# Attention: the scalar engine rounds the output weights in its first slots, the pool keeps their remainders, and the bias is added in pieces of 512 columns

## The chip, the cores and the metric

The kernel runs on one core of one Trainium2 chip. The metric is the device time of one execution in microseconds (us). Five engines work beside one another and meet only at semaphores: PE (matrix multiply), DVE (vector), ACT (scalar), POOL (GpSimd) and SP, which here only issues transfers. Runs of this kernel differ among themselves by about 0.7%.

## The reference, cut to what matters

Two layers, each an attention part and a feed-forward part, on a tensor of 16 batches x 128 rows x 512 columns in float32. The change lies in the attention of layer 1, which comes third of the four parts:

```
q      = rms_norm(x @ q_w + q_b, nq_s)            # 16 heads of 128 columns
k      = rms_norm(ctx @ ki_w + ki_b, nki_s)
v      = ctx @ vi_w + vi_b
attn   = softmax(q k^T / sqrt(128))               # for each batch and head, 128 x 128
x      = x + (attn v) @ o_w + o_b                 # o_w is 2048 x 512
```

The context is shorter than the 257 rows that the reference cuts off as image context, so the text part of it is empty and only the image part is computed.

## The kernel before, in words

Each part of the network is a `Phase`: it allocates its buffers, gives every engine its own program, and ends at a barrier of all engines. The queries, keys and values lie in device memory when the phase `attend` begins (function `attend`, from L2521); the output weights `raw` (16 heads, each 128 x 512) and the bias `obias`, spread over the 128 partitions, are already on the core.

`attend` does 64 steps. Step n = 4*it + j is one head of one group of four batches (`it` runs over 16 quads: four groups g times four quads of heads; j is the head in the quad). What a step does on each engine, and which line it has in the profile:

- DVE `keys` (L2715) scales the keys of a head by a column and by a row, from three buffers on the core; PE `score` (L2793) makes the scores of four batches into a bank; DVE `peak` takes the maximum (L2722) and multiplies it by -rq (L2725, 128 x 4).
- ACT `softmax` (L2675) makes four exponentials of 128 x 128 with their sums; DVE `divide` takes reciprocals (L2732) and scales the probabilities (L2734, 128 x 512).
- PE `turn_prob` (L2801) transposes them, ACT `turned` (L2682) copies them out, PE `mix` (L2812) multiplies with the values.
- The mixed rows are split in a rounded leading part `ol` by ACT `head` (L2688) and the remainder `ot` by DVE `rest` (L2739). PE `output` multiplies them with the output weights in three passes (L100 to L102, twelve matmuls of 512 columns for one batch and one quad), and DVE `add` (L2749) adds the result to `x`.

The stages run displaced, by hand: in the program for step n, PE does transpose(n), mix(n-1), scores(n+2), output(n-5); DVE does add(n-6), keys(n+3), divide(n+1), peak(n+2), rest(n-1); ACT does exponentials(n+1), leading part(n-1), copy(n). Every engine takes its instructions strictly in the order written, and each buffer between two of them is double, so an engine can run at most about two steps ahead. In steps 0 to 4 there is no output to multiply yet.

The weights need the same split, `wol` (rounded, FP32R) and `wot` (the remainder). Before the change POOL does all of it: `cut(i)` is a TENSOR_SCALAR times 1.0 (L2642), then a TENSOR_TENSOR subtraction (L2644), for 16 heads. After four cuts POOL adds the bias to the four batches of group 0 in one instruction of 2048 columns (L2650), then come twelve cuts, then the bias of the three other groups. PE waits for `wo_ready` (four cuts each) ahead of the first output of a quad, and DVE waits for `bias_done` ahead of the first add of a group. The first output is in step 5, the first add that needs the bias of group 1 in step 22.

Of the kernel before, what the change touches and what calls it, by code (L numbers as in the profile page):

```python
# [20 lines left out]
ALU = mybir.AluOpType  # L21
ACT = mybir.ActivationFunctionType
AX = mybir.AxisListType.X

P = 128
B, S, D = 16, 128, 512
T = B * S
C = D // P
GB = 4
# [32 lines left out]
class Phase:  # L62
# [15 lines left out]
    def sb(self, name, shape, dt=F32):  # L78
        return self.stack.enter_context(self.nc.sbuf_tensor(f"{self.name}_{name}", shape, dt))

    def sem(self, name):
        self.sems.append(self.nc.alloc_semaphore(name=f"{self.name}_{name}"))
        return self.sems[-1]
# [2437 lines left out]
def attend(nc, K, A, q_dram, k_dram, v_dram, rq, rk_dram):  # L2521
# [7 lines left out]
    with Phase(nc, "attend") as ph:  # L2529
        sb, sem = ph.sb, ph.sem  # L2530
        raw = A.raw
        wol = sb("wol", [P, H1, D], F32R)
# [4 lines left out]
        kcol, qcol, vbias, obias = A.kcol, A.qcol, A.vbias, A.obias  # L2537
# [8 lines left out]
        wol_done, wo_ready, rkb_loaded = sem("wol_done"), sem("wo_ready"), sem("rkb_loaded")  # L2546
        bias_done, col_done = sem("bias_done"), sem("col_done")
# [6 lines left out]
        def group(it):  # L2554
            return it >> 2 if isinstance(it, int) else within(nc, it >> 2, G - 1)

        def quad_of(it):
            return it & 3 if isinstance(it, int) else within(nc, it & 3, QUADS - 1)
# [4 lines left out]
        def blocks(eng, body):  # L2563

            body(0, 0)
            body(1, 1)
            with eng.Fori(1, IT // 2 - 1) as i:
                body(i * 2, 0)
                body(i * 2 + 1, 1)
            body(IT - 2, 0)  # L2570
            body(IT - 1, 1)

        def ahead(it, par, j, d, step):

            q, k = divmod(j + d, 4)
            if not isinstance(it, int) or 0 <= it + q < IT:
                step(it + q, (par + q) % 2, k)
# [61 lines left out]
        @block.gpsimd  # L2639
        def _(pool):  # L2640
            def cut(i):
                nc.gpsimd.tensor_scalar(wol[:, i], raw[:, i], 1.0, None, ALU.mult).then_inc(wol_done, 1)  # L2642
                pool.wait_ge(wol_done, i + 1)
                ins = nc.gpsimd.tensor_tensor(wot[:, i], raw[:, i], wol[:, i].bitcast(F32), ALU.subtract)  # L2644
                if i % 4 == 3:
                    ins.then_inc(wo_ready, 1)

            def bias(g):
                xg = K.x[:, g * GB:(g + 1) * GB, :]
                nc.gpsimd.tensor_tensor(xg, xg, obias[:].unsqueeze(1).broadcast_to([P, GB, D]), ALU.add  # L2650
                                        ).then_inc(bias_done, 1)

            for i in range(4):
                cut(i)
            bias(0)
            for i in range(4, H1):
                cut(i)
            pool.wait_ge(wo_ready, QUADS)
            pool.sem_inc(wo_ready, IT - QUADS)
            for g in range(1, G):  # L2660
                bias(g)

        @block.scalar
        def _(act):
            for first in (exp_done, probT_done,):
                act.sem_inc(first, FIRST)
            nc.scalar.activation(K.scrap[:], K.ones[:, 0:1], ACT.Exp)

            def softmax(it, j):
                n, g = it * 4 + j, group(it)  # L2670
                act.wait_ge(max_done, n + 1)
                ph.hold(act, held_act)

                for b in range(GB):
                    ins = nc.scalar.activation(prob[:, j % 2, b, :], ps[:, j % 2, b * S:(b + 1) * S], ACT.Exp,  # L2675
                                               bias=row[:, j % 2, 1, b:b + 1], scale=rq[:, bass.ds(g * GB + b, 1)],
                                               accum_out=row[:, j % 2, 2, b:b + 1])
                ins.then_inc(exp_done, 1)

            def turned(it, j):  # L2680
                act.wait_ge(prob_T, it * 4 + j + 1)
                nc.scalar.activation(probT[:, j % 2, :], ps[:, 2 + j % 2, :], ACT.Copy).then_inc(probT_done, 1)  # L2682

            def head(it, par, j):
                act.wait_ge(mixed, it * 4 + j + 1)
                ph.hold(act, held_act)

                nc.scalar.activation(ol[:, par, j, :], ps[:, 4 + j % 2, :], ACT.Identity,  # L2688
                                     bias=vbias[:, bass.ds(quad_of(it) * 4 + j, 1)]).then_inc(ol_done, 1)

            def body(it, par):
                for j in range(4):
                    ahead(it, par, j, 1, lambda i, p, k: softmax(i, k))
                    ahead(it, par, j, -1, head)
                    turned(it, j)

            softmax(0, 0)
            blocks(act, body)
            head(IT - 1, 1, 3)
            row_stats.root(act)  # L2700
# [292 lines left out]
```

## Time and profile before

| | us |
|---|---|
| median of three runs | 1539.83 |
| lowest and highest of them | 1533.41, 1544.79 |
| the profiled execution: time | 1534.74 |
| the profiled execution: span | 1532.3 |
| phase `attend` in it, first instruction to last matmul | about 1120 to 1471 |
| POOL at work in that phase | 1120.2 to 1190.9 |

The profile gives, for one execution, every instruction with start and length; a line in brackets behind an instruction is the idle time of the engine before it and who ended it. PE is busy for 90% of the span, DVE for 55%, ACT for 49%, POOL for 28%. Since the phases stand one after the other, what matters in one phase is how long that phase lasts. The start of `turn_prob` (L2801) in each step is a good clock of the phase: below, T(n) is the start of the first transpose of step n.

### The profile page before, as it was taken

How to read it: one execution, taken by the hardware profiler on the slowest of the kernel's cores; microseconds unless marked ns; L12 is line 12 of the kernel's file. 1: busy time of each engine (PE TensorE's matmuls, PEld its weight loads, DVE VectorE, ACT ScalarE, POOL GpSimd, SP SyncE). 2: the span in 40 equal slices, each digit the busy share in tenths (PEclk: the TensorE clock that was granted, in tenths of full speed). 3: DMA queues.
4: the chain of work that ended last, by engine and by line, in shares of the span. 5: the costliest groups of instructions: out<-in, count | busy, mean ns of one | idle time of the engine just before them, and what ended most of it. 6: DMA issues, size and time to landing. Idle time of an engine off the chain costs nothing. (4 is left out here: it accounts for less than half of the span.)

```text
span 1532.3 us, 26058 instructions
## 1 busy us (share of the span) xinstructions
PE 1377.8 (90%) x7406; PEld 1141.4 (74%) x7407; DVE 836.0 (55%) x1544; ACT 754.1 (49%) x1845; POOL 424.1 (28%) x367
## 2 busy tenths in 40 slices
PE   6899998999898969979999939999958899999968
PEld 5786676888787758857886627878857788888856
DVE  2432322367667875444444247723259777777673
ACT  4222223588678745125555534545435565666520
POOL 0110102236364800539922043020079000000004
PEclk9999998799999977989999969999979999999988
DMA  6998245887787610356645775463445455555202
GB/s 233 356 352 316 108 138 180 290 274 253 234 265 264 220 56 28 137 173 202 195 140 162 246 235 159 144 234 131 160 131 156 144 156 164 159 165 156 70 35 110
DMA packets 171764, 280.91 MB, mean 183 GB/s; under 512 B 29664, under 2 KB 64224, under 8 KB 171424
## 3 DMA queue, kind: packets, MB, share of 16 engines
q1 hardware_dynamic: 146832, 227.58, 46.4%
q0 software_dynamic: 7712, 26.22, 5.1%
q10 hardware_dynamic: 17136, 26.09, 4.6%
q8 instruction: 40, 0.66, 0.2%
q14 instruction: 44, 0.36, 0.1%
HBM read 173.14 MB, written 106.70 MB: 183 GB/s over the span
## 5 line engine op out<-in xcount | busy, mean ns | idle before, releaser
L2675 ACT ACTIVATE attend_prob<-banks,attend_row,rq 128x128 f32<-128x128 f32 x256 | 113.7, 454 | 68.9 <-DVE attend_row L2725 68.9
L100 PE MATMUL banks<-of_shared_split,heads_wl 128*128 (+1 forms) x256 | 108.5, 424 | 17.4 <-ACT heads_ksq L944 12.2
L100 PE MATMUL banks<-of_shared_split,of_ctx_lead 128*128 128x512 f32 x256 | 106.2, 415 | 9.3 <-DVE of_ctx_trail L419 5.5
L100 PE MATMUL banks<-attend_wol,attend_ol 128*128 (+1 forms) x256 | 105.6, 413 | 0.0
L100 PE MATMUL banks<-of_x_lead,queries_wl 128*128 128x512 f32 x256 | 101.9, 398 | 3.8 <-ACT queries_sq L2342 2.3
L102 PE MATMUL banks<-of_shared_split,heads_wt 128*128 (+1 forms) x256 | 103.2, 403 | 0.0
L102 PE MATMUL banks<-of_shared_split,of_ctx_trail 128*128 128x512 f32 x256 | 103.2, 403 | 0.0
L101 PE MATMUL banks<-of_shared_split,of_ctx_lead 128*128 128x512 f32 x256 | 102.9, 402 | 0.0
L2884 POOL TENSOR_TENSOR x_kept<-x_kept,ternary_bias 128x2048 f32 x4 | 18.2, 4594 | 305.6 <-DVE ternary_trail L1298 305.6
L101 PE MATMUL banks<-of_shared_split,heads_wl 128*128 (+1 forms) x256 | 102.6, 401 | 0.0
L101 PE MATMUL banks<-of_x_trail,queries_wl 128*128 128x512 f32 x256 | 101.1, 395 | 0.0
L102 PE MATMUL banks<-of_x_lead,queries_wt 128*128 128x512 f32 x256 | 101.0, 395 | 0.0
L102 PE MATMUL banks<-attend_wol,attend_ot 128*128 (+1 forms) x256 | 100.5, 393 | 0.0
L101 PE MATMUL banks<-attend_wot,attend_ol 128*128 (+1 forms) x256 | 100.1, 391 | 0.0
L2414 DVE TENSOR_TENSOR queries_total<-queries_total,queries_sq 128x512 f32<-128x512 f32 x60 | 41.7, 696 | 91.4 <-ACT queries_sq L2342 91.3
L2338 ACT ACTIVATE queries_head<-banks,queries_bias 128x512 f32<-128x512 f32 x64 | 44.0, 688 | 96.1 <-PE banks L102 84.1
L1053 DVE TENSOR_TENSOR heads_total<-heads_total,heads_ksq 128x512 f32 (+1 forms) x64 | 60.7, 948 | 54.0 <-ACT heads_ksq L944 53.7
L892 ACT ACTIVATE heads_dec<-mlstm_gmax,mlstm_nat 128x128 f32<-128x128 f32 x264 | 83.3, 389 | 5.8 <-POOL mlstm_gmax L794 5.8
L2749 DVE TENSOR_TENSOR x_kept<-x_kept,banks 128x512 f32 (+1 forms) x64 | 43.9, 686 | 67.7 <-PE banks L102 65.0
L2688 ACT ACTIVATE attend_ol<-banks,of_attend_vbias 128x512 fp32r<-128x512 f32 x64 | 44.0, 688 | 73.7 <-PE banks L2812 73.5
L1160 PEld LDWEIGHTS banks<-heads_ctx,heads_cmat 128*128 128x128 f32 x512 | 72.0, 210 | 8.6 <-POOL heads_ctx L803 3.1
L2793 PE MATMUL banks<-attend_kn,attend_q 128*128 128x128 f32 x512 | 70.9, 284 | 5.4 <-DMA attend_q<-q_heads 5.4
(329 smaller groups left out, 3635.8 us busy)
## 6 DMA issues: line engine op xcount, KB each, us to landing
mlstm_gmax<-running_max SPq DMA_DIRECT2D x36, 512.0 KB, 5.8
heads_raw<-in_L_xattn_ki_w SPq DMA_DIRECT2D x32, 512.0 KB, 6.0
k_heads<-heads_key ACTq DMA_DIRECT2D x64, 256.0 KB, 4.2
q_heads<-queries_head SPq DMA_DIRECT2D x64, 256.0 KB
attend_q<-q_heads SPq DMA_DIRECT2D x64, 256.0 KB
of_attend_k<-k_heads SPq DMA_DIRECT2D x60, 256.0 KB, 4.1
of_attend_v<-v_heads SPq DMA_DIRECT2D x60, 256.0 KB, 3.2
sorted_rows<-values_zeros SPq DMA_DIRECT2D x2, 5120.0 KB, 18.2
```

What stands on the lines that cost most here:

```text
L100: nc.tensor.matmul(out, lead_l, lead_r, start=first, stop=False)
L101: nc.tensor.matmul(out, lead_l, trail_r, start=False, stop=False)
L102: return nc.tensor.matmul(out, trail_l, lead_r, start=False, stop=last)
L892: ins = nc.scalar.activation(dec[:, n % 2, b], gmax[:, h // 2 % 4, h % 2 * N + b * S:h % 2 * N + (b + 1) * S], ACT.Exp, scale=-1.0, bias=M ...
L1053: nc.vector.tensor_tensor(t, t, ksq[:, m % 2, :], ALU.add).then_inc(total_done, 1)
L1160: ins = nc.tensor.matmul(ps[:, n // 2 % 2, at:at + DH0 + 1], cmat[:, n % RING, b, :], ctx1[:, bass.ds(half(g), 1), b, n, :].rearrange("p a ...
L2338: nc.scalar.activation(head[:, u % HEADS_RING, :], ps[:, u % 4, :], ACT.Identity, bias=bias[:, h:h + 1]).then_inc(head_done, 1)
L2414: nc.vector.tensor_tensor(t, t, sq[:, u % 2, :], ALU.add).then_inc(total_done, 1)
L2675: ins = nc.scalar.activation(prob[:, j % 2, b, :], ps[:, j % 2, b * S:(b + 1) * S], ACT.Exp, bias=row[:, j % 2, 1, b:b + 1], scale=rq[:, b ...
L2688: nc.scalar.activation(ol[:, par, j, :], ps[:, 4 + j % 2, :], ACT.Identity, bias=vbias[:, bass.ds(quad_of(it) * 4 + j, 1)]).then_inc(ol_do ...
L2749: nc.vector.tensor_tensor(xb, xb, ps[:, 6 + b % 2, :], ALU.add).then_inc(acc_done, 1)
L2793: ins = nc.tensor.matmul(ps[:, j % 2, s], q[:, j, s], kn[:, j % 2, s], start=True, stop=True)
```

## The change

ACT makes the rounded weights: four of them behind the load of its function table, ahead of its first exponentials; two at the end of each of steps 0 to 3; one at the end of each of steps 4 to 7. POOL waits for each and makes only the remainders. The bias is added in 16 instructions of 512 columns each instead of four of 2048; its semaphore is still raised once for each group.

```diff
         @block.gpsimd
         def _(pool):
             def cut(i):
-                nc.gpsimd.tensor_scalar(wol[:, i], raw[:, i], 1.0, None, ALU.mult).then_inc(wol_done, 1)
                 pool.wait_ge(wol_done, i + 1)
                 ins = nc.gpsimd.tensor_tensor(wot[:, i], raw[:, i], wol[:, i].bitcast(F32), ALU.subtract)
                 if i % 4 == 3:
                     ins.then_inc(wo_ready, 1)
 
             def bias(g):
-                xg = K.x[:, g * GB:(g + 1) * GB, :]
-                nc.gpsimd.tensor_tensor(xg, xg, obias[:].unsqueeze(1).broadcast_to([P, GB, D]), ALU.add
-                                        ).then_inc(bias_done, 1)
+                for b in range(g * GB, (g + 1) * GB):
+                    ins = nc.gpsimd.tensor_tensor(K.x[:, b, :], K.x[:, b, :], obias[:], ALU.add)
+                ins.then_inc(bias_done, 1)
...
+            def weight_lead(i):
+                nc.scalar.activation(wol[:, i], raw[:, i], ACT.Copy).then_inc(wol_done, 1)
+
             def body(it, par):
                 for j in range(4):
                     ahead(it, par, j, 1, lambda i, p, k: softmax(i, k))
                     ahead(it, par, j, -1, head)
                     turned(it, j)
-
+                    if isinstance(it, int) and it < 2:
+                        for i in ((4 + 2 * j, 5 + 2 * j), (12 + j,))[it]:
+                            weight_lead(i)
+
+            for i in range(4):
+                weight_lead(i)
             softmax(0, 0)
             blocks(act, body)
```

ACT at the start of `attend`, before the change (the exponentials are the row `attend_prob`, eight of them for steps 0 and 1):

```order
L2667 ACT_TABLE_LOAD
L2667 ACTIVATE scrap<-ones 128x1
L2675 ACTIVATE attend_prob,attend_row<-banks,attend_row,rq 128x128 x8
L2682 ACTIVATE attend_probT<-banks 128x512
L2675 ACTIVATE attend_prob,attend_row<-banks,attend_row,rq 128x128 x4
L2688 ACTIVATE attend_ol<-banks,of_attend_vbias 128x512
L2682 ACTIVATE attend_probT<-banks 128x512
L2675 ACTIVATE attend_prob,attend_row<-banks,attend_row,rq 128x128 x4
```

The same place now (lines below the edit have moved by up to seven):

```order
L2666 ACT_TABLE_LOAD
L2666 ACTIVATE scrap<-ones 128x1
L2691 ACTIVATE attend_wol<-of_attend_raw 128x512 x4
L2674 ACTIVATE attend_prob,attend_row<-banks,attend_row,rq 128x128 x8
L2681 ACTIVATE attend_probT<-banks 128x512
L2691 ACTIVATE attend_wol<-of_attend_raw 128x512 x2
L2674 ACTIVATE attend_prob,attend_row<-banks,attend_row,rq 128x128 x4
L2687 ACTIVATE attend_ol<-banks,of_attend_vbias 128x512
L2681 ACTIVATE attend_probT<-banks 128x512
L2691 ACTIVATE attend_wol<-of_attend_raw 128x512 x2
```

Four rounded weights now stand ahead of the first exponentials, and two behind each copy `attend_probT` of the first four steps.

POOL's whole program of the phase before began with these rows (alternating in this way for all 16 heads):

```order
L2642 TENSOR_SCALAR attend_wol<-of_attend_raw 128x512
L2644 TENSOR_TENSOR attend_wot<-of_attend_raw,attend_wol 128x512
L2642 TENSOR_SCALAR attend_wol<-of_attend_raw 128x512
L2644 TENSOR_TENSOR attend_wot<-of_attend_raw,attend_wol 128x512
L2642 TENSOR_SCALAR attend_wol<-of_attend_raw 128x512
L2644 TENSOR_TENSOR attend_wot<-of_attend_raw,attend_wol 128x512
L2642 TENSOR_SCALAR attend_wol<-of_attend_raw 128x512
L2644 TENSOR_TENSOR attend_wot<-of_attend_raw,attend_wol 128x512
L2650 TENSOR_TENSOR x_kept<-x_kept,of_attend_obias 128x2048
L2642 TENSOR_SCALAR attend_wol<-of_attend_raw 128x512
L2644 TENSOR_TENSOR attend_wot<-of_attend_raw,attend_wol 128x512
```

and is now, in full:

```order
L2643 TENSOR_TENSOR attend_wot<-of_attend_raw,attend_wol 128x512 x4
L2649 TENSOR_TENSOR x_kept<-x_kept,of_attend_obias 128x512 x4
L2643 TENSOR_TENSOR attend_wot<-of_attend_raw,attend_wol 128x512 x12
L2649 TENSOR_TENSOR x_kept<-x_kept,of_attend_obias 128x512 x12
```

The 16 instructions L2642 are gone from POOL; all that is left there are instructions with two input tensors, and none is longer than 512 columns.

## Rows read from the trace of the kernel before

**Rows 1.** The page: busy time, share and count of each engine.
```profile
PE 1377.8 (90%) x7406; PEld 1141.4 (74%) x7407; DVE 836.0 (55%) x1544; ACT 754.1 (49%) x1845; POOL 424.1 (28%) x367
```

**Rows 2.** Waits, 1120 to 1475: waiter, releaser, total us, times, longest.
```profile
PE banks L2801 <- DVE attend_prob L2734: 19.6, 8, 5.1
```

**Rows 3.** Windows: stretch, length, busy PE, PEld, DVE, ACT, POOL; PE clock; DMA.
```profile
1180.00:1190.00 10.00, 5.20 (x32) 4.35 (x32) 9.96 (x6) 2.93 (x10) 10.00 (x3) 1.00 0.18 57
1300.00:1400.00 100.00, 100.00 (x645) 88.84 (x644) 72.94 (x142) 60.83 (x200) 0.00 (x0) 1.00 0.58 160
```

**Rows 4.** Timeline of PE, transposes of steps 0,1,2,5,6,9 to 12: start, us, idle before.
```profile
1130.22 1.09 PE L2801 MATMUL banks<-ident,attend_prob 128*128 128x128 f32 x4 [2.95 <-DVE attend_prob L2734]
...
1137.95 1.11 PE L2801 MATMUL banks<-ident,attend_prob 128*128 128x128 f32 x4 [4.93 <-DVE attend_prob L2734]
...
1143.02 1.08 PE L2801 MATMUL banks<-ident,attend_prob 128*128 128x128 f32 x4 [0.54 <-DVE attend_prob L2734]
...
1154.42 0.66 PE L2801 MATMUL banks<-ident,attend_prob 128*128 128x128 f32 x4 [1.35 <-DVE attend_prob L2734]
...
1159.47 0.60 PE L2801 MATMUL banks<-ident,attend_prob 128*128 128x128 f32 x4
...
1174.46 0.60 PE L2801 MATMUL banks<-ident,attend_prob 128*128 128x128 f32 x4
...
1182.09 0.66 PE L2801 MATMUL banks<-ident,attend_prob 128*128 128x128 f32 x4 [2.50 <-DVE attend_prob L2734]
...
1192.35 1.12 PE L2801 MATMUL banks<-ident,attend_prob 128*128 128x128 f32 x4 [5.06 <-DVE attend_prob L2734]
...
1198.70 0.60 PE L2801 MATMUL banks<-ident,attend_prob 128*128 128x128 f32 x4
```

**Rows 5.** Timeline of DVE: instructions that lie beside POOL's.
```profile
1126.59 0.23 DVE L2725 SCALAR_TENSOR_TENSOR attend_row<-attend_row,rq 128x4 f32<-128x4 f32 x1
1126.74 0.74 DVE L2715 SCALAR_TENSOR_TENSOR attend_kn<-of_attend_k,of_attend_kcol,of_attend_rkb 128x512 f32<-128x512 f32 x1
...
1130.80 1.09 DVE L2725 SCALAR_TENSOR_TENSOR attend_row<-attend_row,rq 128x4 f32<-128x4 f32 x1
1131.81 5.07 DVE L2715 SCALAR_TENSOR_TENSOR attend_kn<-of_attend_k,of_attend_kcol,of_attend_rkb 128x512 f32<-128x512 f32 x1
...
1177.18 4.85 DVE L2734 TENSOR_TENSOR attend_prob<-attend_prob,attend_row 128x512 f32<-128x512 f32 x1
...
1182.67 3.81 DVE L2725 SCALAR_TENSOR_TENSOR attend_row<-attend_row,rq 128x4 f32<-128x4 f32 x1
```

**Rows 6.** Timeline of POOL, same stretches.
```profile
1126.19 1.49 POOL L2642 TENSOR_SCALAR attend_wol<-of_attend_raw 128x512 fp32r<-128x512 f32 x1
...
1130.58 1.29 POOL L2644 TENSOR_TENSOR attend_wot<-of_attend_raw,attend_wol 128x512 fp32r<-128x512 f32 x1
1131.83 4.50 POOL L2650 TENSOR_TENSOR x_kept<-x_kept,of_attend_obias 128x2048 f32<-128x2048 f32 x1
...
1181.45 9.49 POOL L2650 TENSOR_TENSOR x_kept<-x_kept,of_attend_obias 128x2048 f32<-128x2048 f32 x2
```

**Rows 7.** Groups, 1200 to 1475, POOL idle: count, busy us, mean ns, idle before.
```profile
L2734 DVE TENSOR_TENSOR attend_prob<-attend_prob,attend_row 128x512 f32<-128x512 f32 x51 | 35.3, 691 | 1.7
L2725 DVE SCALAR_TENSOR_TENSOR attend_row<-attend_row,rq 128x4 f32<-128x4 f32 x50 | 8.1, 162 | 3.6 <-DVE attend_row L2722 1.1
```

**Rows 8.** Timeline of ACT: phase start; a later step's exponentials; rounding in another phase.
```profile
1120.29 1.28 ACT L2667 ACT_TABLE_LOAD   x1 [1.59 <-PEq L76]
...
1126.94 0.46 ACT L2675 ACTIVATE attend_prob<-banks,attend_row,rq 128x128 f32<-128x128 f32 x1 [5.15 <-DVE attend_row L2725]
...
1155.29 0.46 ACT L2675 ACTIVATE attend_prob<-banks,attend_row,rq 128x128 f32<-128x128 f32 x1 [0.87 <-DVE attend_row L2725]
...
319.99 0.63 ACT L928 ACTIVATE heads_wl<-heads_raw 128x512 fp32r<-128x512 f32 x1 [0.22 <-issue]
```

**Rows 9.** Groups, 364 to 510: another addition of 512 columns on POOL.
```profile
L839 POOL TENSOR_TENSOR x_kept<-x_kept,heads_sq 128x512 f32 x10 | 14.9, 1506 | 0.0
```

## The prediction, made before the changed kernel ran

> **What bounds the kernel now.** I read the page first: PE is busy for 90% of the span [rows 1], so only time in which PE stands still can be won. The change touches one phase, so the next view is the table of windows over that phase. From 1200 on PE is full (100.00 of 100.00 us) at the full granted clock, which is 2.4 GHz, while DVE has 27 us in 100 to spare and POOL does nothing [rows 3]; nothing can be won there. In 1180 to 1190 it is the other way round: PE 5.20, DVE 9.96, POOL 10.00 of 10 us [rows 3]. The list of waits names one wait of PE that matters: for the scaled probabilities of DVE, eight times, 19.6 us in all, the longest 5.1 [rows 2].
>
> The timeline of PE shows where. With T(n) the start of the transposes of step n [rows 4]: T(0) 1130.22, T(1) 1137.95, T(2) 1143.02, T(5) 1154.42, T(6) 1159.47, T(9) 1174.46, T(10) 1182.09, T(11) 1192.35, T(12) 1198.70. So a step takes (1154.42 - 1143.02)/3 = 3.80 us where no output is multiplied yet. That is the loop peak, exponentials, divide, next peak, over DVE and ACT; PE waits in it. It takes (1174.46 - 1159.47)/3 = 5.00 us where PE multiplies the output too and is itself the bound. Two stretches stand out: T(0) to T(2) and T(9) to T(12).
>
> The timelines of DVE and POOL, laid side by side, say why. An instruction of DVE with two inputs on the core stands still while POOL runs one with two inputs. The keys L2715 take 0.74 alone, but 5.07 from 1131.81, beside a bias of 4.50 from 1131.83: 4.33 of blocking, nearly its whole length. L2734 takes 0.69 alone [rows 7] and 4.85 from 1177.18; L2725 takes 0.16 alone [rows 7] and 3.81 from 1182.67 [rows 5, 6]. Beside the subtraction of 1.29 from 1130.58, L2725 takes 1.09 from 1130.80: it ends when that does, so a subtraction blocks for about 1.15. Beside the TENSOR_SCALAR from 1126.19, the keys from 1126.74 take their plain 0.74, and L2725 from 1126.59 takes 0.23, 0.07 more than alone [rows 5, 6]: an instruction of DVE that starts 0.4 to 0.6 us into the one-input instruction is hardly held up by it. So what hurts most is the bias, and what the change takes off POOL is the milder half of a cut.
>
> **The change, part by part.**
>
> *The late biases, T(9) to T(12).* Before: 1198.70 - 1174.46 = 24.24 us against three steps at 5.00, so 9.24 lost. The last part of it is PE's clock: after PE stood idle 5.06 us the four transposes of step 11 took 1.12 against 0.60 or 0.66, the lower level of 1.2 GHz. After: twelve pieces. The nearest row for a piece is the POOL addition of 512 columns of another phase, 1.51 us in the mean [rows 9]; a quarter of the bias of 4.50 would be 1.13 [rows 6]. I take 1.26, near the subtraction's 1.29 of the same size in the same phase. Does DVE get in between two pieces? Two biases ran back to back from 1181.45, and the L2734 that had waited since 1177.18 ended at 1182.03, 0.58 into the first of them [rows 5, 6]; so the one that waits is served at the border, and POOL starts again behind it. In each step DVE has three instructions with two such inputs (L2715, L2734, L2725; 0.74 + 0.69 + 0.16 = 1.59 together), and it is busy for 72.94% of 5.00 = 3.65 us [rows 3]. So 2.06 us of other work, which is not blocked, lies beside the three pieces that start behind them: 3 x 1.26 - 2.06 = 1.7 of waiting a step. With it DVE takes 5.35, 0.35 over PE's 5.00, for the 3.6 steps that twelve pieces last (12 x 1.26 = 15.1, and 0.6 to 0.8 a step while POOL itself waits): 1.3 us. Ahead of it stands slack: at T(10) a block of 4.16 cost PE only 7.63 - 5.00 = 2.63, so 1.5 us were absorbed, which covers that. I take a loss of 0.5; the ends are 0, and three full waits of 1.26 in 3.6 steps, 3.6 x (3.65 + 3.78 - 5.00) - 1.5 = 7.2. **Term: -8.7** (-9.2 to -2.0).
>
> *Up to T(0).* ACT is idle for 5.15 us ahead of its first exponential [rows 8], and four roundings of 0.63, as the copy of that kind and size in another phase takes [rows 8], are 2.5: nothing. POOL's first subtraction waits for the table load, which ends at 1121.57 [rows 8], the scrap of 0.2 and one rounding: it starts at about 1122.4, some 2 us behind POOL's start before. From there one subtraction follows the other to 1127.6, then four pieces to about 1132.7. The L2725 of step 0, from 1126.59, fell beside a TENSOR_SCALAR and will fall beside a subtraction (+0.9 of its 1.15), and the first L2734 meets a piece (+0.2 over what it met before). **Term: +1.1** (0 to two full blocks, +2.3).
>
> *T(0) to T(1).* Before 7.73, since the keys stood 4.33 us behind the bias [rows 4, 5]. The keys now find a piece of 1.26, most of it beside the exponentials, and L2725 waits 0.5. I take 4.4: **-3.3**. The ends: the free step of 3.80 (-3.9), and three full waits, 3.80 + 3.8 = 7.6 (-0.1).
>
> *T(1) to T(5).* Before 1154.42 - 1137.95 = 16.47, of it 5.07 for the first step (tail of the same jam) and three times 3.80. Two things come here. ACT has 0.87 us idle ahead of the exponentials of a 3.80 step [rows 8] and gets two roundings, 1.26: up to +0.4 in each of four steps, unless the step is longer anyway. POOL gets both subtractions of a step at once, when ACT has done its roundings, about when DVE does L2725. The first then meets the keys, which lie beside the exponentials and have time; the second follows the keys and meets L2734, which is in the loop: 0 to 1.15, I take 0.5. PE is partly at its lower clock here (the transposes of steps 0 to 2 take 1.08 to 1.11 [rows 4]), which lengthens the scores that the loop may wait for; I don't add it, since it lies beside the others. A step is then 3.80 + 0.2 + 0.5 = 4.5. 4 x 4.5 = 18.0: **+1.5**. The ends: four free steps, 15.2 (-1.3); two full subtractions in each, 4 x (3.80 + 2.58) = 25.5 (+9.0).
>
> *Steps 5 to 8.* One rounding and one subtraction a step. The loop needs 3.80 and the PE 5.00, so 1.15 of blocking fits. Nothing. The waits for the weights are covered: the first output is in step 5, its four cuts are done by 1127.5; quad 3 is first used in step 17, its cuts are done in step 8. The same for the bias of group 1 (first needed in step 22, done by about step 12). SP's queue is not touched.
>
> Sum: -8.7 + 1.1 - 3.3 + 1.5 = **-9.4 us**, with ends of -14.4 and +9.2. The profiled execution took 1534.74 and would take 1525.3. It stands 5.1 below the median of 1539.83; from the median it is 1530.4. I give 1530.
>
> **A rule weighed against the rows.** The row of the keys beside the TENSOR_SCALAR showed 0.74, no blocking. The Trainium skill ("SBUF — State Buffer", section "SBUF: two separate sides") says that DVE and GpSimd share one pair of ports under an exclusive lock, and that a GpSimd instruction that reads SBUF keeps it for the whole instruction against a DVE instruction with two SBUF inputs. With the bias and the subtraction the trace agrees (4.33 of 4.50, about 1.15 of 1.29); with the TENSOR_SCALAR it does not. By the page every cut would have held DVE for 1.49 + 1.29 = 2.78 us before and 1.29 after, so the third and fifth terms could only fall; by the rows two subtractions in a step block more than the mixed pair did. I go by the rows; the other reading is rival A.
>
> **The rivals.**
>
> *A, the start gets shorter too.* If POOL's pair of subtractions slips beside the exponentials as the mixed pair did, steps 1 to 4 keep 3.80: sum -9.2 + 0.5 - 3.9 - 1.3, about -14, or -12 with half of it. Time 1526 to 1528. For it: the cuts before cost next to nothing at 3.80. Against it: they held DVE only about half as long. The page above speaks for it. 13%.
>
> *B, the late pieces still jam DVE.* With pieces of 1.51, as the nearest addition took [rows 9], and 3.0 of waiting a step, DVE takes 6.65, which is 1.65 x 3.6 = 5.9 over PE's pace, less 1.5 of slack: 4.4 lost. That makes -9.2 + 4.4 - 0.7 = -5.5, and -4.1 if PE's clock falls again (step 11 and 12 lost 1.4 by it: 6.35 against 5.00 [rows 4]): 1534 to 1536. Against it: the other work of DVE covers part of each wait. 22%.
>
> *C, slower.* The two subtractions of a step enter the loop in full, because POOL now starts in a burst right behind ACT rather than in its own rhythm: +9.0 in T(1) to T(5) with +2.3 ahead, -0.1, and half of the late gain kept (-4.6). That is +6.6, 1546. It decides from where a step of that stretch takes over 6.0. Against it: the first of the pair meets the keys, which have time. 9%.
>
> *D, nothing to be seen*, -2 to +2, from a start that costs 7: inside B's and C's ranges, counted there.
>
> That leaves 56% for the forecast, -6 to -12.
>
> **How the numbers follow.** The three runs of before lie 11 us apart, so about 1% (15 us) is what a measurement of this kernel can tell from no change. The largest gain that the rows allow, 14.4, is under it, so faster by over 1% needs rival A and luck in the runs: 0.11. Slower by over 1% needs rival C at its end and beyond: 0.04. Within 1%: 0.85. Range: from rival A counted from the profiled execution, 1534.74 - 14.4 = 1520, to rival B counted from the median with the spread of a few us on top, 1541; it leaves out C and the tails.
>
> **What would show each step.** The list of waits: L2801 for L2734 from 19.6 us to about 9. The longest L2715, L2734 and L2725 under 2.5 us each, where they were 5.07, 4.85 and 3.81. T(9) to T(12) near 15.5. T(0) about 1 us later, T(1) near 1135.7, T(5) near 1154, T(12) near 1189. POOL's work over by about 1186, with busy time of 40 instead of 70. A L2734 over 1.3 us in each of steps 1 to 4 would confirm the second subtraction; T(1) to T(5) under 16 is rival A, over 21 rival C; windows of PE under 9 in 10 after T(8) are rival B. Wrong altogether: if the keys, L2734 and L2725 stay over 3 us, the border between two pieces does not let DVE in.

## The result, and the profile after

Over 20 runs of each kernel the change takes 1534.26 us (1525.84 to 1544.45) against 1539.24 (1533.41 to 1547.26): a ratio of 0.9962, 95% interval 0.9945 to 0.9979, or 5.9 us less (3.2 to 8.5); the two medians alone lie 5.0 apart. A second series, of twelve runs, gave 0.9933 (0.9905 to 0.9961). The kernel is faster, by less than 1%. The forecast was 1530, between 1520 and 1541.

The execution of the change that was profiled took 1544.45 us, more than the median of before. Its phase `attend` began at 1135.80 (table load of ACT), where it had begun at 1120.29: 15.5 us were lost ahead of the first changed instruction, by the differences between runs. So the two spans can't be compared, but the phases can. All times of phases below are counted from P, the start of that table load: T(63)-P, the start of the last transposes, was 332.0 before and is 326.6 after, 5.4 less. In these two executions that is what the change does; what a phase gains differs from trace to trace, as the table below shows.

The page after, the same waits as in [rows 2], and the windows from P to T(63) of both kernels, before first (columns as in [rows 3]):

```profile
PE 1387.7 (90%) x7406; PEld 1149.7 (75%) x7407; DVE 833.6 (54%) x1544; ACT 762.8 (49%) x1861; POOL 396.5 (26%) x363
```

```profile
PE banks L2808 <- DVE attend_prob L2741: 15.7, 8, 7.6
```

```profile
1120.29:1452.30 332.01, 308.92 (x1957) 274.64 (x1958) 248.98 (x440) 193.53 (x639) 69.13 (x36) 0.97 0.53 149
```

```profile
1135.80:1462.40 326.60, 307.29 (x1957) 272.79 (x1958) 243.91 (x440) 201.67 (x655) 43.70 (x32) 0.97 0.54 151
```

POOL's busy time falls from 69.1 to 43.7 us, ACT's grows by 8.1 (16 roundings), and DVE's falls by 5.1 though it does the same: DVE's "busy" holds time in which it stands blocked. PE's longest wait for the scaled probabilities has grown, from 5.1 to 7.6.

PE's transposes after, which answer to [rows 4] (steps 0, 1, 2, 5, 6, 9, 10, 11, 12):

```profile
1150.78 1.11 PE L2808 MATMUL banks<-ident,attend_prob 128*128 128x128 f32 x4 [7.61 <-DVE attend_prob L2741]
1154.51 0.66 PE L2808 MATMUL banks<-ident,attend_prob 128*128 128x128 f32 x4 [0.91 <-DVE attend_prob L2741]
1158.89 0.66 PE L2808 MATMUL banks<-ident,attend_prob 128*128 128x128 f32 x4 [1.93 <-DVE attend_prob L2741]
...
1171.98 0.66 PE L2808 MATMUL banks<-ident,attend_prob 128*128 128x128 f32 x4 [0.20 <-DVE attend_prob L2741]
1177.34 0.60 PE L2808 MATMUL banks<-ident,attend_prob 128*128 128x128 f32 x4
...
1192.31 0.60 PE L2808 MATMUL banks<-ident,attend_prob 128*128 128x128 f32 x4
1197.87 0.66 PE L2808 MATMUL banks<-ident,attend_prob 128*128 128x128 f32 x4 [0.43 <-DVE attend_prob L2741]
1203.72 0.66 PE L2808 MATMUL banks<-ident,attend_prob 128*128 128x128 f32 x4 [0.65 <-DVE attend_prob L2741]
1208.75 0.60 PE L2808 MATMUL banks<-ident,attend_prob 128*128 128x128 f32 x4
```

T(9) to T(12) went from 24.24 to 16.44. T(0)-P went the other way, from 9.93 to 14.98. DVE's rows say why (they answer to [rows 5]; the first is step 0, the others lie beside the late pieces):

```profile
1142.23 5.57 DVE L2732 SCALAR_TENSOR_TENSOR attend_row<-attend_row,rq 128x4 f32<-128x4 f32 x1
...
1188.40 1.84 DVE L2722 SCALAR_TENSOR_TENSOR attend_kn<-of_attend_k,of_attend_kcol,of_attend_rkb 128x512 f32<-128x512 f32 x1
...
1190.36 1.58 DVE L2741 TENSOR_TENSOR attend_prob<-attend_prob,attend_row 128x512 f32<-128x512 f32 x1
...
1192.70 0.40 DVE L2732 SCALAR_TENSOR_TENSOR attend_row<-attend_row,rq 128x4 f32<-128x4 f32 x1 [0.16 <-DVE attend_row L2729]
```

and POOL's beside them, which answer to [rows 6]:

```profile
1137.89 5.01 POOL L2643 TENSOR_TENSOR attend_wot<-of_attend_raw,attend_wol 128x512 fp32r<-128x512 f32 x4 [82.19 <-ACT attend_wol L2691]
1142.85 4.93 POOL L2649 TENSOR_TENSOR x_kept<-x_kept,of_attend_obias 128x512 f32<-128x512 f32 x4
...
1187.19 17.60 POOL L2649 TENSOR_TENSOR x_kept<-x_kept,of_attend_obias 128x512 f32<-128x512 f32 x12 [0.18 <-POOLq L2658]
```

The small L2732 of step 0 was asked for at 1142.23, in the last remainder, and ended at 1147.80, with the last of the four pieces (1142.85 + 4.93 = 1147.78). It was let in at none of the four borders between; this is the lock-out of what follows. Beside the late pieces, each of the three instructions waits for one border only: 1.1, 0.9 and 0.2 us.

### The profile page after: what moved, and what is told of

It reads as the page before. It is cut to its first block and busy times, and to the rows that moved or that the text cites. A ratio compares the mean times of both kernels' runs of the same rounds, so it can differ in the third digit from the quotient of the medians.

```text
span 1542.4 us, 26070 instructions
## 1 busy us (share of the span) xinstructions
PE 1387.7 (90%) x7406; PEld 1149.7 (75%) x7407; DVE 833.6 (54%) x1544; ACT 762.8 (49%) x1861; POOL 396.5 (26%) x363
## 5 line engine op out<-in xcount | busy, mean ns | idle before, releaser
L100 PE MATMUL banks<-of_shared_split,heads_wl 128*128 (+1 forms) x256 | 110.2, 430 | 20.3 <-ACT heads_ksq L944 15.4
L101 PE MATMUL banks<-of_shared_split,heads_wl 128*128 (+1 forms) x256 | 104.0, 406 | 0.0
L1043 DVE TENSOR_TENSOR heads_wt<-heads_raw,heads_wl 128x512 fp32r<-128x512 f32 x64 | 60.1, 939 | 31.4 <-ACT heads_wl L928 31.0
```

The lines of the kernel that those rows point to most:

```text
L100: nc.tensor.matmul(out, lead_l, lead_r, start=first, stop=False)
L101: nc.tensor.matmul(out, lead_l, trail_r, start=False, stop=False)
L1043: nc.vector.tensor_tensor(wt[:, m % 2], raw[:, m // 2 % 2, :, (m % 2) * P:(m % 2 + 1) * P], wl[:, m % 2].bitcast(F32), ALU.subtract).then_ ...
```

## The experiments

The theory from these rows: the pieces win T(9) to T(12); the start loses 5 us because DVE can be shut out over a whole series of POOL instructions that follow each other without a gap; the roundings on ACT bring nothing. Twelve more traces, one table. T(0)-P is the time up to the first transposes, T(63)-P the whole phase, all in us. T(16) to T(63) is the same in all but e6 and e8 and shows how well traces compare:

| kernel | T(0)-P | T(0) to T(5) | T(5) to T(9) | T(9) to T(16) | T(16) to T(63) | T(63)-P |
|---|---|---|---|---|---|---|
| before | 9.93 | 24.20 | 20.04 | 44.21 | 233.62 | 332.0 |
| e12 before again | 9.93 | 24.22 | 20.02 | 45.35 | 233.62 | 333.1 |
| the change | 14.98 | 21.20 | 20.33 | 36.40 | 233.65 | 326.6 |
| e1 change again | 10.60 | 22.21 | 21.64 | 36.41 | 233.65 | 324.5 |
| e10 change again, timed | 10.58 | 21.51 | 20.16 | 36.41 | 233.65 | 322.3 |
| e4 waits between pieces | 14.97 | 21.87 | 21.67 | 36.44 | 233.64 | 328.6 |
| e2 whole bias | 14.57 | 21.20 | 25.11 | 39.66 | 233.65 | 334.2 |
| e11 bias first | 10.45 | 21.53 | 20.15 | 36.45 | 233.65 | 322.2 |
| e7 POOL held at start | 10.16 | 22.87 | 21.72 | 36.42 | 233.65 | 324.8 |
| e3 pieces only | 9.91 | 22.23 | 20.22 | 36.82 | 233.65 | 322.8 |
| e9 pieces only, timed | 9.93 | 21.71 | 20.04 | 35.87 | 233.62 | 321.2 |
| e6 gated, POOL rounds | 10.69 | 21.17 | 20.00 | 36.38 | 234.66 | 322.9 |
| e8 gated at the wrong place | 10.45 | 23.42 | 21.09 | 40.14 | 234.71 | 329.8 |
| e5 gated | 9.26 | 19.61 | 20.03 | 34.92 | 233.65 | 317.5 |

**e1, the change once more.** No edit.

> The changed kernel once more, for the start of the phase attend. With P the start of the table load of ACT in the phase and T(n) the start of the transposes of step n, the first trace had T(0)-P 14.98 us, because the first L2732 of DVE, asked for at 1142.23, ran only when all four pieces of the first bias were through (5.57 us). Theory A (POOL keeps the ports over back-to-back instructions at this place, every time): L2732 again over 5 us, T(0)-P about 15. Rival B (chance of arrival: as in all other places DVE is let in at the first border): L2732 under 1.3 us and T(0)-P about 11. T(12)-P: 73 by A, 69 by B.

B, at this place: L2732 took 0.94, T(0)-P 10.60. But e2 and e4, run beside it, which begin on POOL with the same four remainders, had it shut out again. So the start of the change has two outcomes. e4 and e1 asked for L2732 at the same 6.18 us after P and had the fourth remainder from 5.83 and 5.82 on. In e1 it went in at the border:

```profile
1135.47 0.94 DVE L2732 SCALAR_TENSOR_TENSOR attend_row<-attend_row,rq 128x4 f32<-128x4 f32 x1
1136.34 1.83 DVE L2722 SCALAR_TENSOR_TENSOR attend_kn<-of_attend_k,of_attend_kcol,of_attend_rkb 128x512 f32<-128x512 f32 x1
```

and in e4 (L2733 there) at none:

```profile
1130.79 5.81 DVE L2733 SCALAR_TENSOR_TENSOR attend_row<-attend_row,rq 128x4 f32<-128x4 f32 x1
1136.53 0.74 DVE L2723 SCALAR_TENSOR_TENSOR attend_kn<-of_attend_k,of_attend_kcol,of_attend_rkb 128x512 f32<-128x512 f32 x1
```

T(12)-P was 70.9, between the 73 and 69 of the two: there is a second toss, PE's clock. The windows of step 5, e1 first (6.66 us) and then e10 (5.18), show PE's granted clock at 0.74 and 1.00 (last but two columns):

```profile
1162.10:1168.76 6.66, 6.66 (x32) 6.12 (x33) 5.58 (x9) 4.87 (x17) 2.59 (x2) 0.74 0.63 161
```

```profile
1157.46:1162.64 5.18, 5.18 (x33) 4.56 (x33) 4.37 (x8) 3.67 (x12) 1.29 (x1) 1.00 0.71 190
```

PE stands idle for 1.8 to 2.2 us ahead of each of steps 2 to 4 in the trace of the change, and in every trace but that of e10 it is at the lower level (1.2 GHz) for a stretch somewhere in steps 1 to 5; what that costs depends on where. In the trace of the change the stretch lies in step 4, where the granted clock was 0.60 and PE had time to spare:

```profile
1167.72 1.11 PE L2808 MATMUL banks<-ident,attend_prob 128*128 128x128 f32 x4 [2.15 <-DVE attend_prob L2741]
```

That step took no longer (4.26). In e1, e4 and e7 it lies in step 5, the first in which PE is itself the bound, and cost 1.5 to 1.6 us against e10. In e1 and e4 PE was at the lower level in step 1 as well (granted clock 0.50 in e1, 1.00 in e10), and step 2 took 4.96 in place of 4.24, 0.7 us that came with it. So the phase is 322.3 with neither toss against it (e10), 324.5 with the clock alone (e1), 326.6 with the lock-out alone (the change), 328.6 with both (e4).

**e2, the bias whole again.** In `bias(g)`:

```diff
-                for b in range(g * GB, (g + 1) * GB):
-                    ins = nc.gpsimd.tensor_tensor(K.x[:, b, :], K.x[:, b, :], obias[:], ALU.add)
-                ins.then_inc(bias_done, 1)
+                xg = K.x[:, g * GB:(g + 1) * GB, :]
+                nc.gpsimd.tensor_tensor(xg, xg, obias[:].unsqueeze(1).broadcast_to([P, GB, D]), ALU.add
+                                        ).then_inc(bias_done, 1)
```

> The changed kernel with the bias of a group in one instruction of 2048 columns again; the roundings stay on ACT. By my theory the pieces are what wins T(9) to T(12), so that stretch goes back to 22 to 25 us from 16.4. The start: if POOL keeps the ports until its queue of instructions is empty (A), T(0)-P stays about 15; if DVE is let in ahead of the bias (B), T(0)-P is 11 and T(0) to T(1) is 7 to 8. Total against the changed kernel: +6 to +8 us. A rival says that taking the roundings off POOL is what wins; then the total stays within 2 us of the changed kernel.

334.2, 7.6 over the change with the same lock-out at the start: the forecast size. So the roundings alone, with the bias whole, are 1 to 2 us slower than the kernel before, the lock-out included, by one trace of it and two of before. The jam came back, one step earlier than before because POOL is done with its cuts sooner; so T(9) to T(12) (19.7) misses what I said, and T(8) to T(12) shows it, 29.7 against 21.4. PE in step 9 (idle 4.81) and DVE beside the biases:

```profile
1191.46 1.12 PE L2808 MATMUL banks<-ident,attend_prob 128*128 128x128 f32 x4 [4.81 <-DVE attend_prob L2741]
```

```profile
1186.63 4.78 DVE L2741 TENSOR_TENSOR attend_prob<-attend_prob,attend_row 128x512 f32<-128x512 f32 x1
...
1192.16 3.65 DVE L2732 SCALAR_TENSOR_TENSOR attend_row<-attend_row,rq 128x4 f32<-128x4 f32 x1 [0.16 <-DVE attend_row L2729]
```

**e3 and e9, pieces only.** In the kernel before; e9 is the same kernel, timed beside e10, the change.

```diff
-                xg = K.x[:, g * GB:(g + 1) * GB, :]
-                nc.gpsimd.tensor_tensor(xg, xg, obias[:].unsqueeze(1).broadcast_to([P, GB, D]), ALU.add
-                                        ).then_inc(bias_done, 1)
+                for b in range(g * GB, (g + 1) * GB):
+                    ins = nc.gpsimd.tensor_tensor(K.x[:, b, :], K.x[:, b, :], obias[:], ALU.add)
+                ins.then_inc(bias_done, 1)
```

> The kernel before with only the bias cut in pieces; POOL still makes roundings and remainders in turn. Theory: T(0)-P as before (9.9, since DVE gets in beside the roundings), T(0) to T(1) about 4.5 instead of 7.7, T(1) to T(5) about 15.5, T(9) to T(12) about 16.5 instead of 24.2: T(12)-P about 67, against 78.4 before and 72.9 with the change, so better than the whole change by some 5 us. Rival: the roundings on POOL prolong its work so that the pieces meet DVE as badly; T(12)-P over 72.

> The kernel before with only the bias in pieces, the kernel of e3 once more, timed. In the traces its phase attend (T(63)-P) took 322.8 us against 332.0 before and 324.5 to 328.6 with the whole change. Theory: the pieces are all of the gain and the roundings on ACT cost 2 to 4 us: ratio to before 0.994 (-9 us), at or under that of the change. Rival (the roundings on ACT contribute): ratio over that of the change by 0.002 or more.

322.8 and 321.2 us of phase, against 322.3 to 328.6 with the whole change; measured ratios to before 0.9901 (0.9864 to 0.9937) for the pieces alone and 0.9933 (0.9905 to 0.9961) for the change beside it. Both ratios rest on the same runs of before, so their overlap does not settle which kernel is better. Run against run, the pieces alone were the shorter in 62 of 72 pairs (medians 1524.62 and 1529.54), which chance alone gives in 1 to 2 of 100 cases: the roundings on ACT cost time here. By the traces they cost it mainly where DVE is shut out; without that the phases are alike (322.3 in e10 against 322.8 and 321.2). T(12)-P in e3 was 68.3 where I had said 67, since steps 0 to 5 still took 22.2. T(9) to T(12) says little here: POOL's late pieces come later, and what they cost falls on steps 11 and 12 (5.88 and 5.86 in e3), of which step 12 lies outside that stretch.

**e4, waits between the pieces.** In the loop of `bias(g)`:

```diff
+                    pool.wait_ge(wol_done, 4)
                     ins = nc.gpsimd.tensor_tensor(K.x[:, b, :], K.x[:, b, :], obias[:], ALU.add)
```

> The changed kernel with a wait of POOL on a semaphore that is long there ahead of each piece of the bias. If DVE was shut out in the first bias because the pieces follow each other without a gap (A), the first L2732 falls from 5.57 to under 1.5 us and T(0)-P to about 11. If the gap does not matter (rival), it stays over 5. T(9) to T(12) within 0.5 us of 16.4 in both cases.

The rival came: 5.81. A wait that is already met makes no gap; the pieces start 1.22 us apart with it as without it.

**e10, the change timed.** No edit.

> The changed kernel beside e9 on the same chip. Theory: ratio 0.996; in its trace DVE's first L2732 is either shut out over the whole series of eight back-to-back POOL instructions (over 5 us, T(0)-P about 15) or let in at the first border (under 1 us, T(0)-P 10.6), nothing in between.

Let in (0.83), ratio 0.9933 where I had 0.996. In five traces that begin with four remainders and the bias (the change, e1, e2, e4, e10) L2732 took 5.1 to 5.8 us three times and 0.8 to 0.9 twice, and nothing lay between. The blocking also goes the other way: where DVE is let in, POOL's next piece takes 1.71 in place of 1.26, 0.45 longer (here the second piece of e10).

```profile
1133.63 1.71 POOL L2649 TENSOR_TENSOR x_kept<-x_kept,of_attend_obias 128x512 f32<-128x512 f32 x1
```

**e11, bias first.**

```diff
+            bias(0)
             for i in range(4):
                 cut(i)
-            bias(0)
```

> The changed kernel with the four pieces of the first bias ahead of the first four remainders. The pieces need no rounding, so POOL starts at once, beside the first two keys. If DVE can be shut out over any back-to-back series (theory), the keys or the first L2732 may wait up to 5 us, T(0)-P between 10 and 16, and the long wait ends within 0.1 us of the last POOL instruction of the series. If only the change of kind from remainder to piece does it (rival), no wait over 1.3 us and T(0)-P 10 to 12.

The rival's numbers came: the two first keys took 3.38 in place of 1.42, about 1.0 of waiting each, L2732 took 0.72, and T(0)-P was 10.45. But DVE is let in by chance too, in two of five of the traces above, so one run does not show that the order of the kinds decides. What makes POOL keep the ports stays open.

**e7, POOL held at the start.** Ahead of POOL's first cut:

```diff
+            pool.wait_ge(max_done, 1)
             for i in range(4):
                 cut(i)
```

> The changed kernel with one wait ahead of POOL's first instruction, until DVE's first L2732 is done. The first trace of the change and two of three experiments had DVE shut out over all back-to-back instructions there (5.1 to 5.8 us). Theory: with POOL idle at that moment the first L2732 takes 0.2 and is never shut out; the first four remainders and pieces move some 4.5 us later, onto steps 0 to 2. T(0)-P 10 to 11 instead of 15. T(63)-P about 323 to 325. Rival (DVE gets shut out by the next back-to-back series in the same way): one of keys, scaling or L2732 over 4 us in steps 0 to 2.

The theory held: no wait over 1.1 us anywhere, T(0)-P 10.16, T(63)-P 324.8, which includes the dip of the clock in step 5 (6.76). The gain at the start is given back in part in steps 0 to 4 (22.9), where now every scaling waits about 0.5.

**e5, gated.** POOL's program becomes a list: four cuts, four pieces, twelve cuts, twelve pieces, each behind DVE's L2732 of one step; ACT's roundings 4 to 15 spread over steps 0 to 7.

```diff
-            for i in range(4):
-                cut(i)
-            bias(0)
...
+            for m, step, i in plan:
+                pool.wait_ge(max_done, m + 1)
+                step(i)
...
-                        for i in ((4 + 2 * j, 5 + 2 * j), (12 + j,))[it]:
+                        for i in ((4 + j,), (8 + 2 * j, 9 + 2 * j))[it]:
```

> The changed kernel, with each POOL instruction of the phase held back until DVE has just finished the L2732 (here by its line of this kernel) of a certain step: one a step, from step 0 to 30 (two in step 9); ACT makes its roundings 4 to 15 one, then two a step. Theory (an instruction of POOL costs only if it meets L2732 or the scaling of the probabilities; behind L2732 it meets only the keys, which have time): T(0)-P 9.4, steps 0 to 4 about 3.85, T(9) to T(12) 15.0, T(63)-P about 318 against 332.0 before, 326.6 in the first trace of the change and 324.5 in the second: about -14 us against before. Rival (each POOL instruction costs the same wherever it starts, or POOL's late work costs outputs): T(63)-P not under 323.

317.5, forecast 318. It has the shortest phase of all and the lowest ratio, 1519.24 us against 1538.93, 0.9885 (0.9841 to 0.9929, from four runs; the interval overlaps that of the pieces alone). DVE in it, one step of 3.73 us, with POOL's piece behind it:

```profile
1148.84 0.69 DVE L2742 TENSOR_TENSOR attend_prob<-attend_prob,attend_row 128x512 f32<-128x512 f32 x1
1149.45 0.68 DVE L2730 TENSOR_REDUCE attend_row<-banks 128x4 f32<-128x512 f32 x1
1150.17 0.16 DVE L2733 SCALAR_TENSOR_TENSOR attend_row<-attend_row,rq 128x4 f32<-128x4 f32 x1
1150.25 0.74 DVE L2747 SCALAR_TENSOR_TENSOR attend_ot<-banks,of_attend_vbias,attend_ol 128x512 fp32r<-128x512 f32 x1
1150.91 1.32 DVE L2723 SCALAR_TENSOR_TENSOR attend_kn<-of_attend_k,of_attend_kcol,of_attend_rkb 128x512 f32<-128x512 f32 x1
```

```profile
1150.41 1.28 POOL L2648 TENSOR_TENSOR x_kept<-x_kept,of_attend_obias 128x512 f32<-128x512 f32 x1 [2.45 <-DVE attend_row L2733]
```

The piece takes DVE 0.6 us, on the keys (1.32 for 0.74), beside ACT's exponentials, where it costs nothing.

**e8, gated at the wrong place.** Against e5:

```diff
-                pool.wait_ge(max_done, m + 1)
+                pool.wait_ge(exp_done, FIRST + m + 1)
```

> As the gated kernel, but each POOL instruction is released by the end of ACT's exponentials instead of DVE's L2732, so that it starts just ahead of the scaling of the probabilities. Theory: the scaling waits about 1.0 in every step and it lies in the loop, so steps 0 to 4 take 4.7 to 4.9 instead of 3.85; from step 5 on PE is the bound and the wait is absorbed; T(63)-P 4 to 5 us over the gated kernel. Rival: placement is indifferent, within 1 us of the gated kernel.

POOL now starts 0.17 us ahead of the scaling, which takes 1.65 for 0.69:

```profile
1156.51 1.65 DVE L2742 TENSOR_TENSOR attend_prob<-attend_prob,attend_row 128x512 f32<-128x512 f32 x1
```

```profile
1156.34 1.26 POOL L2648 TENSOR_TENSOR x_kept<-x_kept,of_attend_obias 128x512 f32<-128x512 f32 x1 [3.42 <-ACT attend_prob L2675]
```

Steps 0 to 4 took 4.69 each against 3.92 in the mean in e5. The same instructions cost 3.8 us more there, and 1.2 more up to T(0), by where they start: together 5.0, where 4 to 5 was forecast. The total is 12.3 over e5, because my list held POOL's work so late that others waited for it. In step 6 DVE's first add waited 2.73 us for the first bias (1.0 us lost), and in steps 9, 13 and 17 PE waited for weights (4.1, 1.2 and 1.1 us lost). Step 9 took 9.05 us, with 2.21 idle ahead of its output and a granted clock of 0.81:

```profile
1188.57 0.50 PE L100 MATMUL banks<-attend_wol,attend_ol 128*128 x1 [2.21 <-issue]
```

The first part is the test; the second is a flaw of the list.

**e6, gated, with POOL rounding.** The kernel before with the list of e5. Against e5:

```diff
             def cut(i):
+                nc.gpsimd.tensor_scalar(wol[:, i], raw[:, i], 1.0, None, ALU.mult).then_inc(wol_done, 1)
                 pool.wait_ge(wol_done, i + 1)
...
-                        for i in ((4 + j,), (8 + 2 * j, 9 + 2 * j))[it]:
-                            weight_lead(i)
...
-            for i in range(4):
-                weight_lead(i)
```

> The same holding back, but in the kernel before, with POOL making both rounding and remainder of each weight and the bias in pieces; ACT has nothing added. Theory: the remainder now starts 1.6 us behind L2725 and can meet the scaling of the probabilities, +0 to +0.5 in four steps: T(63)-P 318 to 320. If moving the roundings to ACT was worth anything, this kernel is over 2 us slower than the gated one with ACT; if not, within 2.

322.9, 5.4 over e5 where 318 to 320 was forecast; ratio 0.9915 (0.9883 to 0.9948), which overlaps that of e5. Of the 5.4, 3.0 lie up to T(5) and belong to the test. The remainder of a weight now starts 2.0 us later than POOL's release (1.6 in step 3), into the scaling (POOL, then DVE):

```profile
1142.29 1.92 POOL L2642 TENSOR_SCALAR attend_wol<-of_attend_raw 128x512 fp32r<-128x512 f32 x1 [1.43 <-DVE attend_row L2726]
1144.30 1.28 POOL L2644 TENSOR_TENSOR attend_wot<-of_attend_raw,attend_wol 128x512 fp32r<-128x512 f32 x1
```

```profile
1144.44 1.70 DVE L2735 TENSOR_TENSOR attend_prob<-attend_prob,attend_row 128x512 f32<-128x512 f32 x1
```

The other 2.4 are the flaw of e8 again: PE waited for weights in steps 9 and 17 (1.18 and 0.78 idle ahead of the output).

```profile
1186.20 0.49 PE L100 MATMUL banks<-attend_wol,attend_ol 128*128 x1 [1.18 <-issue]
```

So with this list the rounding on ACT is worth about 3 us at the start. A list that gates POOL's rounding and its remainder apart, so that each remainder starts right behind L2732, was not tried and could make up for it.

**e12, before again.**

> The kernel before once more, since all gains are counted from one trace of it. Theory (its phase is set by the order of the instructions, not by chance): T(63)-P within 1.5 us of 332.0, with the jams again at T(0) to T(1) (7.7) and T(9) to T(12) (24.2). Rival: its first trace was a bad one like the first of the change, and T(63)-P is 327 or less; then the gain of every kernel here is smaller by as much.

333.1, with both jams (7.73 and 25.4; step 11 took 7.49 instead of 6.35, with PE's granted clock at 0.66 instead of 0.78). The base of the comparison holds.

## Why the prediction was right or wrong

*What bounds the phase, and the late biases: right.* Forecast for T(9) to T(12) -8.7, measured -7.8: 1.44 us were lost where I took 0.5, since steps 9 and 10 took 0.56 and 0.85 over their 5.00. Both parts of that term were a little off. DVE waited 2.0, 2.2 and 2.3 us in steps 8 to 10 where I had 1.7 a step, which with its 3.65 of work is 2.4 us over PE's pace and not 1.3. About 1.0 of that was absorbed, not 1.5: I had read the slack from the one block of 4.16, but DVE waited 5.05 in all in that step of the kernel before. e2 confirms the cause: with the bias whole the jam is back, 7.6 us.

*T(0) to T(1): right where DVE was let in*, 4.06 and 4.07 in e10 and e1, where I had 4.4 and the keys did meet a piece (1.82 and 1.83). The 3.73 of the change's own trace is luck: the pieces were over by then, and the keys ran at 0.74. *T(1) to T(5): near*, 17.47 in the trace of the change and 17.45 in e10 where I had 18.0; 18.1 in e1 and e4, at PE's lower clock. The mechanism (two remainders at once, the second onto the scaling) is in the rows, but at +0.4 in every second step and with L2732 as often its victim. The sign that I had set for it, a scaling of over 1.3 us in each of steps 1 to 4, did not come: in the change's trace the longest took 1.09.

*Up to T(0): wrong in the first trace.* I gave +1.1 with an upper end of +2.3 and measured +5.05. The step that failed is "the one that waits is served at the border". I took it from one border, between two biases, and it holds for every wait of the late pieces (none over 1.1 us); but at the start of the phase it failed in three of five traces. The Trainium skill ("SBUF — State Buffer", section "SBUF: two separate sides") has the lock held for one whole instruction; by that the small L2732 would have waited for the rest of one remainder, 0.7 us. The 0.8 and 0.7 of e1 and e10 agree; the 5.4 of the change does not. Where DVE was let in, the term was +0.65 and the phase 9.7 us shorter (e10, 322.3 against 332.0: -7.8, +0.65, -3.7, +1.0 and +0.1 for the stretches), against -9.4 forecast. The other sign that failed with this step is the list of waits: 15.7 us in place of 19.6, where I had about 9, since 7.6 of it is the wait ahead of T(0). The measured 5.9 lies between that and the 5.4 to 3.4 of the traces with the lock-out (the change, e4). How often each occurs among the untraced runs is not known. That 1534.26 lies within the range is in part luck: the upper end of 1541 was set for late pieces that jam (rival B), and not for a lock-out ahead of T(0).

*Steps 5 to 8: I gave nothing.* 0.1 to 0.3 us in the change and e10, but 1.6 in e1 and e4, nearly all of it in step 5 at PE's lower clock. I had named the clock only for the late jam.

*ACT's idle time:* the roundings start 0.52 us apart (1.17 for two) and fill the pause; behind those of steps 1 and 3 the exponentials follow without one. Where that happens they start 0.24 behind L2732 in place of 0.12, so the cost was under 0.2 a step.

*The rivals.* A (the start gets shorter too) did not come about by itself; e5 shows that it was there to be had, at 14.5 us. The total landed at B's figure (-5.5), but not by B's way: it asked for late waits of 3.0 a step and 4.4 us lost there; they were 2.2 a step, and 1.4 lost. C did not come about, though e8 makes a mild form of it on purpose (4.69 a step, not over 6.0). The roundings, which the change moves to ACT, are not what wins: the pieces win. Moving the roundings was worth something in one comparison alone, 3.0 us where POOL's starts are placed (e6 against e5).

## What to carry to other kernels

Where two engines block each other, count where each instruction of the one starts against the loop of the other, not how long it is in all: the same instructions on POOL cost next to nothing (e5) or 0.8 us more a step (e8). Hold a helper engine back with a semaphore of the engine that it blocks, so that it starts just behind the loop's last critical instruction, and don't let it run a series without gaps ahead of a first critical instruction (holding it back gave T(0)-P 10.16 in e7, against 14.6 to 15.0 in the traces with the lock-out). Such a list must still meet every later deadline: in e6 and e8 it did not, and that cost 2.4 and 7.3 us. When the effect is smaller than the spread of runs, compare a stretch inside the traces from a common point, and take the trace more than once.

## What the hardware showed that I had not expected

DVE's small L2732 (0.16 us) stood 5.1 to 5.8 us behind a series of back-to-back POOL instructions in three traces of five, to the end of the series, from start positions that let it in after 0.7 to 0.8 in the two others. Why is open. A wait on a semaphore that is already met leaves no gap for it (e4, pieces 1.22 us apart with and without). A TENSOR_SCALAR of POOL (1.49 us) holds up two-input instructions of DVE at its start alone: the scaling that began 0.06 us into it took 0.43 longer, the first small instruction of the phase (L2707), at 0.2 us, took 0.27 longer, L2725 at 0.39 us 0.07 longer, and what began later ran at its plain time. And a phase that leaves PE idle 2 us a step falls to the lower clock at a place that differs between executions of one kernel: it cost nothing to be seen in step 4 (the change) and 1.5 us in step 5 (e1).
